# A two-layer conditioned FFN on one core: second z-row buffer, trace adds in pairs, mask on ScalarE, shared part accumulated by DMA

## The reference, cut to what matters

```
ctx    = causal_ema(x, tau_ctx)
gated  = x * sigmoid([x, ctx] @ Wg.T + bg)
mod    = 0.5 + sigmoid(gelu(x @ Wn1.T + bn1) @ Wn2.T + bn2)       # 8 columns
trace_d = causal_ema(gated * mod[d], tau_d)          # d = 0..7
temporal = sum over d of trace_d * blend_w[d]
gate   = sigmoid(temporal @ Wtemp.T + btemp)
soma   = gelu(x @ Wsoma.T + bsoma)
z      = layernorm((soma * gate) @ Wout.T) * gamma + beta
probs  = softmax(z @ router.T)     # 64 experts, the 8 largest kept, renormalised
routed = sum over the 8 of weight * down(silu(z @ w_gate) * (z @ w_up))
shared = (silu(z @ sg) * (z @ su)) @ ws_down
out    = x + routed + shared
```

## Time and profile before

| | |
|---|---|
| median of 3 runs | 1124.4 us (1123.6 to 1125.13) |
| the profiled execution's own time | 1116.69 us |
| span of the profile, first to last instruction | 1114.9 us |
| mean granted TensorE clock | 0.929 |
| busy over the span | PE 86%, DVE 67%, ACT 41%, POOL 60% |

### The profile page before, as it was taken

The page is one execution under the profiler, slowest core; times in us unless marked ns, Lnnn a source line. Parts: engine busy times, 40 slices in busy tenths (PEclk is TensorE's granted clock), DMA queues, the critical chain, the costliest instruction groups (busy, mean ns, idle before and its releaser), DMA issues.

```text
span 1114.9 us, 14811 instructions
## 1 busy us (share of the span) xinstructions
PE 954.6 (86%) x4524; PEld 668.5 (60%) x4524; DVE 743.1 (67%) x1522; ACT 461.2 (41%) x835; POOL 664.1 (60%) x496
## 2 busy tenths in 40 slices
PE   4968999999999999987379899988586899999960
PEld 2533698899989998863144555544353565556640
DVE  3648566667666766524779999999955786777620
ACT  1330444554455545533455665666421232222320
POOL 2113444555455544407999999999931477777870
PEclk9989999999999999988689999999887799999995
DMA  5869234444354432223212752335168599997557
GB/s 174 281 231 352 58 76 118 90 87 99 76 122 90 92 88 39 30 85 76 96 66 70 240 157 86 91 118 182 44 229 274 143 270 256 257 262 150 91 75 157
DMA packets 89782, 155.46 MB, mean 139 GB/s; under 512 B 12072, under 2 KB 70128, under 8 KB 86576
## 3 DMA queue, kind: packets, MB, share of 16 engines
q1 hardware_dynamic: 48112, 91.27, 25.2%
q0 software_dynamic: 25104, 39.86, 20.6%
q10 hardware_dynamic: 16496, 23.49, 6.2%
HBM read 119.56 MB, written 43.42 MB: 146 GB/s over the span
## 4 chain that ended last, share of the span: by engine, by line
POOL 13%; PE 10%; issue 10%; DMA 9%; DVE 4%; ACT 2%; POOLq 2%; DVEq 1%; ACTq 0%; SPq 0%
DMA odd_rows<-ys,slots 5%; POOL wide L635 4%; PE bank L1662 4%; POOL wide L643 3%; DMA xg<-z_rows,slots 2%; POOL xg L721 2%; POOL out L728 2%; POOL odd_rows L728 2%; DVE wide L1271 1%; PE bank L1739 1%; PE bank L1729 1%; PE bank L1722 1%; ACT zrow L945 1%; DMA z_rows<-zrow 1%; ACT wide L895 1%
## 5 line engine op out<-in xcount | busy, mean ns | idle before, releaser
L635 POOL TENSOR_TENSOR wide<-wide 128x1024 f32<-128x1024 f32 x64 | 156.6, 2461 | 30.8 <-issue 30.6
L1271 DVE TENSOR_TENSOR_SCAN wide<-bank,wide 128x512 f32<-128x512 f32 x128 | 149.3, 1209 | 22.8 <-POOL wide L635 22.6
L871 ACT ACTIVATE h_raw<-bank,b 128x512 f32<-128x512 f32 x128 | 88.1, 689 | 168.1 <-PE bank L1635 165.7
L1208 DVE TENSOR_TENSOR h_lo<-h_raw,h_hi 128x512 fp32r<-128x512 f32 x128 | 87.3, 692 | 91.8 <-ACT h_hi L875 91.8
L1650 PE MATMUL bank<-w_hi,h_hi 128*128 128x256 f32 x512 | 144.4, 282 | 0.1
L1650 PE MATMUL bank<-w_lo,h_hi 128*128 128x256 f32 x512 | 142.1, 278 | 0.0
L1650 PE MATMUL bank<-w_hi,h_lo 128*128 128x256 f32 x512 | 142.0, 277 | 0.0
L609 POOL DMA_INDIRECT x_rows<-ob,put x64 | 110.3, 1723 | 28.3 <-issue 16.0
L643 POOL TENSOR_TENSOR wide<-wide 128x1024 f32<-128x1024 f32 x46 | 108.5, 2359 | 11.9 <-issue 8.1
L895 ACT ACTIVATE wide<-wide,blend 128x512 f32<-128x512 f32 x128 | 84.2, 715 | 59.3 <-POOL wide L635 55.5
L1635 PE MATMUL bank<-ex_hi,w_hi 128*128 128x512 f32 x256 | 99.5, 389 | 2.4 <-issue 2.4
(11 more groups left out here) (239 smaller groups left out, 2041.3 us busy)
## 6 DMA issues: line engine op xcount, KB each, us to landing
wide<-in_mwp SPq DMA_DIRECT2D x40, 512.0 KB, 4.5
wide<-m_rows SPq DMA_DIRECT2D x16, 1024.0 KB, 4.9
w1s<-in_fW SPq DMA_DIRECT2D x8, 1024.0 KB, 5.4
w2s<-in_fW SPq DMA_DIRECT2D x8, 1024.0 KB, 5.3
own<-in_mwp SPq DMA_DIRECT2D x15, 512.0 KB, 4.4
z_rows<-zrow SPq DMA_DIRECT2D x8, 640.0 KB, 7.4
head<-in_mwp SPq DMA_DIRECT2D x9, 512.0 KB, 4.5
xT<-in_xT ACTq DMA_DIRECT2D x8, 512.0 KB, 4.2
```

The source lines that it names most:

```text
L635: G.tensor_tensor(drive[n % DRIVES], gb[d % 2], md[d // HD][:, d % HD, :].unsqueeze(1).to_broadcast([P, CT, S]), ALU.mult).then_inc(c_u, 1)
L871: A.activation(h1_raw[f % 4][:, :], bank[:, 2 + f % 4, :], ACT.Gelu_apprx_tanh, bias=b1_0[:, bass.ds(e, 1), f]).then_inc(b_h, 1)
L1208: V.tensor_tensor(h1_lo[:, f, :], h1_raw[f % 4][:, :], h1_hi[:, f, :].bitcast(F32), ALU.subtract).then_inc(b_lo, 1)
L1271: o = V.tensor_tensor_scan(dst[:, c, :], decay[:, d:d + 1].to_broadcast([P, S]), drive[(D * b + d) % DRIVES][:, c, :], 0.0, ALU.mult, ALU.add)
```

## The change

It replaces these things in the conditioning and in the first and last lines of the expert stage:

1. Traces 3 and 4, and 5 and 6, are added to each other on DVE (`pair_traces`) before one add to `acc`. POOL adds 1, 2, 4, 6, 7 to `acc`; 3 and 5 are gone.
2. `zrow` becomes two buffers, with a store semaphore each. Its rows get 4 more columns (324 instead of 320 values); one of them holds the inverse of the weight sum. DVE writes the unnormalised weights, and the experts multiply by the inverse (`xgT_out`: a product of two single columns instead of a copy).
3. `match_replace` is the end of `pick` on DVE. ACT makes the 0/1 mask from it with `Sign` and `Relu` (`chosen_out`) straight into `mask_all`. The last batch compares on DVE, straight into `mask_all`.
4. The two small TENSOR_SCALARs of `rstd_of` go from POOL to ACT (`moments`).
5. `x1_rows` is gone; layer 0 adds into `out`. ACT copies the shared part, halved, to `ost` (`share_out`), and POOL issues a transfer that adds it to `out` (`rows_add`). `xr`, `row_in`, `row_store` and `finish` are gone.
6. The lists get new orders. POOL: rstd, drive 7, drive 0, add 6, drive 1, add 7, drives 2 and 3, add 1, drive 4, add 2, rows_add(b-3), drives 5 and 6, add 4. DVE: scans 0 and 1, pick, shared_b, ctx_scan, scan 2, gate_soma, scan 3, shared_a, scan 4, pair 4, stats, scan 5, gate_in, scan 6, pair 6, route_weights, scan 7. PE: logits_in and shared_b_in come before x1T_in. ACT: z_out, weighted 2, soma_out, weighted 3, shared_b_out, x1T_out, weighted 4, h1_out, gate_out, shared_out, weighted 5, t8_out, weighted 6, exponentials, chosen_out, moments, weighted 7, wg_out, normalise, weighted 0 and 1, share_out.

The core of the diff:

```diff
-ZW = H + E1
+ZW = H + E1 + 4
-        zrow = sb("zrow", [P, TT, ZW])
+        zrows = [sb(f"zrow{p}", [P, TT, ZW]) for p in range(2)]
+        PAIRED = (4, 6)
+        SUMS = tuple(d for d in range(1, D) if d + 1 not in PAIRED)
             def rstd_of(q):
-                pool.wait_ge(c_mv, level(q))
+                pool.wait_ge(c_mw, level(q))
                 pool.wait_ge(c_no, level(q - 1, TT))
-                G.tensor_scalar(veps1[:, :], mv1[:, :, 1], 4 * EPS, None, ALU.add)
-                G.tensor_scalar(shift1[:, :], mv1[:, :, 0], -1.0, None, ALU.mult)
-                pool.drain()
+            def moments(q):
+                act.wait_ge(c_mv, level(q))
+                act.wait_ge(c_no, level(q - 1, TT))
+                A.activation(veps1[:, :], mv1[:, :, 1], ACT.Copy, bias=4 * EPS)
+                A.activation(shift1[:, :], mv1[:, :, 0], ACT.Copy, scale=-1.0).then_inc(c_mw, 1)
+            def rows_add(q):
+                pool.wait_ge(c_fin, level(q))
+                pool.dma_start(out[q * S:(q + 1) * S, :].rearrange("(t p) c -> p t c", p=P), ost[:, :, :],
+                               accum_op=ALU.add).then_inc(c_ost, 16)
+            def chosen_out(q):
+                act.wait_ge(c_top, level(q))
+                A.activation(rep[:, :, :], rep[:, :, :], ACT.Sign, bias=far[:, :], scale=-1.0)
+                act.drain()
+                A.activation(mask_all[:, :, q * TT:(q + 1) * TT].rearrange("p e t -> p t e"), rep[:, :, :], ACT.Relu).then_inc(c_ma, 1)
+            def share_out(q):
+                act.wait_ge(c_dm, level(q))
+                wait_moved(act, c_ost, q - 1, 16)
+                A.activation(ost[:, :, :], rows4(4), ACT.Copy, scale=0.5).then_inc(c_fin, 1)
+            def pair_traces(b, d):
+                n = (D - 1) * b + d - 1
+                dve.drain()
+                V.tensor_tensor(trace[n % TRACES], trace[n % TRACES], trace[(n - 1) % TRACES], ALU.add).then_inc(c_pair, 1)
+                dve.drain()
             def route_weights(q):
                 dve.wait_ge(c_ex, level(q))
-                V.tensor_tensor(mask[:, :, :], mask[:, :, :], ex[:, :, :], ALU.mult)
+                V.tensor_tensor(zrow[:, :, H:H + E1], ex[:, :, :], chosen(q), ALU.mult)
                 dve.drain()
-                V.tensor_reduce(wsum[:, :], mask[:, :, :], AX.X, ALU.add)
+                V.tensor_reduce(wsum[:, :], zrow[:, :, H:H + E1], AX.X, ALU.add)
                 dve.drain()
-                V.reciprocal(wsum[:, :], wsum[:, :])
-                dve.drain()
-                V.tensor_tensor(zrow[:, :, H:ZW], mask[:, :, :], wsum[:, :].unsqueeze(2).to_broadcast([P, TT, E1]),
-                                ALU.mult).then_inc(c_zr, 1)
+                V.reciprocal(zrow[:, :, H + E1], wsum[:, :]).then_inc(c_zr, 1)
             for e in range(ROWS):
                 e_gather(e)
-            pool.wait_ge(c_ost, level(B - 1, 16))
+            rows_add(B - 1)
+            wait_moved(pool, c_ost, B - 1, 16)
```

More of the change, by code:

```diff
@@ L329, in build @@
         c_no = sem("c_no", TT)
+        c_ma = sem("c_ma")
         c_mst = sem("c_mst", 16)
+        c_zst = [sem(f"c_zst{p}", 16) for p in range(2)]
         c_mdl = [sem(f"c_mdl{n}", 16) for n in range(2)]
+        c_pair, c_mw = sem("c_pair"), sem("c_mw")
         c_pad, e_pad = sem("c_pad", 0), sem("e_pad", 0)
         c_in = [sem(f"c_in{p}", 16) for p in range(2)]
-        c_xr, c_zst, c_ost = sem("c_xr", 16), sem("c_zst", 16), sem("c_ost", 16)
+        c_ost = sem("c_ost", 0)
         (c_Tm, c_x1T, c_ctx, c_wgm, c_wgt, c_gat, c_h1m, c_h1, c_som, c_so, c_u,
@@ L683, in step @@
                     add_trace(b, 2)
-                if on(b):
-                    add_trace(b, 3)
+                if on(b - 3):
+                    rows_add(b - 3)
                 if on(b):
@@ L714, in _ @@
             pool.wait_ge(z_dummy, 16 * 6)
-            pool.wait_ge(c_zst, level(B - 1, 16))
+            for p in range(2):
+                pool.wait_ge(c_zst[p], level(B // 2 - 1, 16))
             def e_gather(e):
@@ L976, in step @@
                     shared_out(B - 2)
+                    moments(B - 1)
                     normalise(B - 1)
+                    share_out(B - 2)
                     return
@@ L983, in step @@
                     z_out(b - 2)
+                if on(b):
+                    weighted(b, 2)
                 if ahead(b):
@@ L986, in step @@
                 if on(b):
[L987 removed]
+                    weighted(b, 3)
+                if on(b - 2):
+                    shared_b_out(b - 2)
                 if ahead(b + 1):
                     x1T_out(b + 1)
[L990 to L991 removed]
                 if on(b):
[L993 removed]
+                    weighted(b, 4)
                 if ahead(b + 1):
@@ L997, in step @@
                     gate_out(b - 1)
-                if on(b):
-                    weighted(b, 4)
+                if on(b - 2):
+                    shared_out(b - 2)
                 if on(b):
                     weighted(b, 5)
-                if on(b - 2):
-                    shared_out(b - 2)
+                if ahead(b + 1):
+                    t8_out(b + 1)
+                if on(b):
+                    weighted(b, 6)
                 if on(b - 2):
                     exponentials(b - 2)
-                if on(b):
-                    weighted(b, 6)
-                if ahead(b + 1):
-                    t8_out(b + 1)
+                    chosen_out(b - 2)
+                if on(b - 1):
+                    moments(b - 1)
                 if on(b):
@@ L1019, in step @@
                     weighted(b + 1, 1)
+                if on(b - 2):
+                    share_out(b - 2)
             def last_step():
@@ L1025, in last_step @@
                 shared_out(B - 1)
+                share_out(B - 1)
             def front_only():
@@ L1267, in scan_unit @@
                     n = (D - 1) * b + d - 1
-                    dve.wait_ge(c_add, level(n - TRACES))
+                    old, of = divmod(n - TRACES, D - 1)
+                    if of + 1 in SUMS and old >= 0:
+                        dve.wait_ge(c_add, added(old, of + 1))
                     dst = trace[n % TRACES]
@@ L1318, in to_exponents, with chosen @@
                 V.tensor_tensor(neg[:, :, :], lgp, top8[:, :, 0:1].to_broadcast([P, TT, E1]), ALU.subtract).then_inc(c_neg, 1)
+            def chosen(q):
+                return mask_all[:, :, q * TT:(q + 1) * TT].rearrange("p e t -> p t e")
             def pick(q):
@@ L1419, in drain_share @@
                 stats(B - 1)
-                finish(B - 2)
             def last_share():
@@ L1431, in last_share @@
                 prep(1, 0)
-                finish(B - 1)
                 prep(1, 1)
@@ L1475, in step @@
                     scan_unit(b, 6)
+                if on(b):
+                    pair_traces(b, 6)
                 if on(b - 2):
-                    finish(b - 2)
+                    route_weights(b - 2)
                 if on(b):
@@ L1481, in front_only @@
             def front_only():
+                for zrow in zrows:
+                    V.memset(zrow[:, :, H + E1 + 1:ZW], 0.0)
+                V.memset(far[:, :], -1.0e38)
                 ctx_scan(0, alpha)
```

105 lines of the change are left out of this document (47 added, 58 removed).

## The result

The changed kernel takes 1131.03 us (median of 6 runs, 1129.67 to 1135.41) where the kernel before took 1123.82 in runs beside it: ratio 1.0096, 95% interval 1.0072 to 1.012. It is about 1% slower; the prediction said 0.6% faster. The profiled execution of the changed kernel took 1131.57 us with a span of 1129.8, 14.9 more than before. Of these 14.9 some belong to the one execution profiled before, which lay 7.7 us under the median of the runs shown with it; the ratio stands for 10.8. In this part a time written as "L1314" belongs to a line of the kernel that the rows are of: in the changed kernel L623 is `drive_of`, L634 the add to `acc` and L638 `rows_add` on POOL, L1297 the scan, L1314 `pair_traces` and L1400 the product of exponentials and mask on DVE.

The account below looks back on a forecast made before the run. It took POOL, full and in the conditioning loop with PE next, as the bound, and POOL's order to carry delays through the experts. Terms -6.6 - 4.0 - 0.2 + 4.6 = -6.2 us from 1124.4 gave 1118.2, range 1114 to 1123.

Parts of the forecast that it names:

- DVE in a steady step: DVE's busy time per conditioning step: from 36.2 us to 35, between 33.7 and 37.5 depending on the pairs' waits.
- The port between DVE and POOL: POOL's blocking by DVE in a conditioning step: plus 0.8 us for a second large add, minus 0.4 for work leaving DVE.
- POOL in a steady step: POOL's conditioning work: one add fewer -2.36, TENSOR_SCALARs -0.6, rows_add +1.5; with the port terms -1.1 us, 37.4 to 36.3.
- PE: PE in a conditioning step: work unchanged, a new wait for ACT's copy against a shorter one before z; near 36 us.
- ACT: ACT in a conditioning step: some 3 us more work beside 14 us of room, costed at nothing.
- Steps: Six conditioning intervals between rstd_of's, each 1.1 us shorter: 6.6 us gained, bounds 0 and 13.
- The first two steps: Start to first rstd_of: drive 3 fills idle time ahead of POOL's first add, one add fewer; gain 4.0 us, bounds 1 and 6.
- The drain: Last batch at the pipeline's end: moments through ACT +0.3, share_out +0.5, less DVE work -1.0; gain 0.2 us.
- The first scatter: Start of the expert stage: POOL waits for the last rows_add to land before gathers 6 and 7 and scatters; 4.6 us lost.
- L: Time from issue to landing of the last rows_add: estimated 6.6 us, between 3.7 and 22.9.
- The line through the two accumulating rows: Landing-time estimate from accumulating transfers of 128 KB (4.9 us) and 4 MB (22.9 us): 4.3 + 4.6 per MB.
- A: Rival: PE's new wait and slow pairs on DVE keep the conditioning step at 37.4 us; 1124.8 us, chance 0.20.

Follow-up runs that it names:

- e7: The kernel before with pairing alone: pair adds on DVE after scans 4 and 6, adds 1, 2, 4, 6, 7 on POOL; 1132.26 us, ratio 1.0093.
- e1: The changed kernel with the pair adds' second input read from PSUM, so traces 3 and 5 miss the sum; 1113.12 us, ratio 0.9938.
- e12: The changed kernel without POOL's drains ahead of adds and in rstd_of, where a semaphore wait replaces it; 1126.98 us, ratio 1.0057.
- e5: e1 with PE transposing the next x ahead of logits and shared part, and ACT's copy moved up to match; 1111.27 us, ratio 0.9912.
- e8: The changed kernel with pairing undone, PE's and ACT's orders of e5 and the early last rows_add of e4; 1123.18 us, ratio 1.0012.
- e9: The changed kernel with the product of batches 0 to 5 on POOL, orders of e5 and early last transfer of e4; 1116.68 us, ratio 0.9971.
- e13: e9 without POOL's drains ahead of adds and in rstd_of; 1108.3 us, ratio 0.9895.
- e15: e5 without POOL's drains ahead of adds and in rstd_of; 1095.9 us, ratio 0.9787.
- e10: The changed kernel with only the orders of e5 and the early last transfer of e4; 1121.08 us, ratio 1.0013.
- e16: The kernel before without POOL's drain ahead of each add to acc, nothing else; 1115.09 us, ratio 0.9968.
- e4: The changed kernel with the last rows_add issued after gather 3 instead of after gather 5; 1127.34 us, ratio 1.005.

## Why the prediction was wrong, point by point

The step that failed is the cost of DVE: the waits of its instructions with two inputs in SBUF were taken too small, and no bound was drawn from DVE's side of the port.

- *DVE in a steady step* is the step that failed. It took 35 us, at most 37.5; the like stretch shows 38.4. Cut at the powers, four steady steps had DVE busy 35.2 to 35.7 us before and 37.6 to 38.1 after: up by some 2.4, where 1.2 down was forecast. Two terms were mis-sized. The pairs were given half a POOL instruction of waiting, and measured 1.7 us each over their own 1.22; by its own words, 33.7 and twice 1.2, the sum would even have been 36.1 and not 35. And the product, which stays on DVE with two inputs in SBUF, was costed at nothing new: only the last product's 1.42 was taken off, as if the first would not change. Its mean was 0.66 us before (580 to 860 us) and is 1.96 now, 2.77 in the step shown. By e7 the pairs alone suffice for the whole loss, and by e1 the loss is gone with their wait. The first product before, 580 to 860 us:

```profile
L1357 DVE TENSOR_TENSOR mask<-mask,ex 128x256 f32<-128x256 f32 x8 | 5.3, 659 | 0.1
```

- *The port between DVE and POOL* had the mechanism and the wrong bill: it charged POOL 0.8 us per add, and let DVE's side of the same event (3.21 for 1.3 us) go as if DVE had room for it. The page that it named, the Trainium skill, "SBUF — State Buffer", section "Who interferes with whom", says that of the two instructions the one issued second blocks until the first ends. The traces agree: 3.05 us for a pair issued 0.39 us into a drive of 2.36. The prediction used that rule only with POOL as the second one.
- *POOL in a steady step* was wrong in what it concluded. Its work fell even more than the 1.1 us forecast, from 35.8 us a step to 33.2, but the saving became idle time ahead of its adds. `rows_add` was priced at 1.5 us; its issue is listed at 1.30, and the drive behind it starts 0.83 after it. The prediction missed that the drain of the next add waits for the landing. In the changed kernel that is nearly hidden (e12), in the orders of e5, e8 and e9 it is not (e13 to e15).
- *PE* was said to stay near 36 us and did (35.7 in 40). But PE's list did cost: in the unpaired kernel PE's and ACT's order is worth 1.5 us a step, in the paired one 1.1 (e8, e10).
- *ACT* held. Its busy time went from 23.0 to 26.0 us a step, Sign took 0.49 us, and there are two table loads a step as before. But POOL's drives, which waited 0.3 us in all before, now wait 12.7 us for `weighted`; in a kernel bound by DVE's waits no run shows that this costs time.
- *Steps*, -6.6 in the forecast, were +11.8: this is nearly the whole error, 18.4 of the 21.1 us between the sum and the profiled difference (17.0 by the ratio).
- *The first two steps*, -4.0, is what the milestone shows, but not by the way given: add 1 still waited 3.29 us, to 526.20, although drive 3 now stood ahead of it. In e12, without the drain, the same add starts at 520.57 with no wait. Without drains the front gains 5 us more (e12, e16), so the drain did hold it, as assumed.
- *The drain* (here the end of the pipeline, not the instruction) was forecast as -0.2 and is +1.1. The last reciprocal came earlier as expected; but gather 0, which waits for the store behind it, came 3.8 us later after that store's issue. SP issued its last weight load 4.0 us ahead of the store before, and 1.1 us now. Over the 18 traces the store took 13.4 to 14.3 us to land where that distance was at most 1.7 us, and 9.7 to 10.7 where it was 3.4 or more; that ties the delay to the loads in flight, though no run changed it alone.
- *The first scatter*: L was put at 6.6 us and is 6.9, the loss 4.6 and 4.5, and e4 takes it back. The line through the two accumulating rows was right. By the Trainium skill, "DMA: Bandwidth & Descriptors", section "Anatomy of one DMA — SWDGE (gpsimd) path", an estimate of L would be 3.2 us; the traces do not agree, with 5.8 us as the shortest of eight.
- Of the rivals, A was right in kind: the bound moved, and it named slow pairs. It took the 37.4 us of before for a floor under the step and did not ask whether the new bound could lie above the old one; so it ended at no change.

## What to carry to other kernels

When two engines block each other as DVE and POOL do here, cost an instruction moved between them with its wait on both sides: its own time plus the rest of the other engine's instruction, and the same again for whoever waits for its result. On the engine near its limit that sum, not the work saved on the other, decides; and work taken out at one place comes back as a longer wait at the next such instruction. A transfer moved onto POOL's own queue made the drain behind it wait for its landing: use semaphores there, or keep a landing's length of other work ahead of the next drain.
